# Scores of causal attention from two float32r parts, heads in pairs over the two partition halves

## What is computed

```
q = query @ wq + query @ Aq @ Bq * 4.0
k = query @ wk
v = query @ wv + query @ Av @ Bv * 4.0
q, k = apply_rope(q), apply_rope(k)
scores = einsum('bhqd,bhkd->bhqk', q, k) / sqrt(16)
scores = where(causal, -1e9, scores)
out = einsum('bhqk,bhkd->bhqd', softmax(scores), v) @ wo
x = layernorm(query + out)
h = butterfly(x @ W_exp + b_exp, up_weights)
h = butterfly(gelu(h + up_bias), down_weights)
x = layernorm(x + h @ W_con + b_con + down_bias)
```

## Time and profile before

| | us |
|---|---|
| median of 3 runs | 1386.56 |
| lowest, highest | 1382.6, 1386.81 |
| the profiled execution, its own time | 1382.2 |
| its span, first to last instruction | 1380.5 |
| TensorE busy | 1235.3 |
| VectorE busy | 1008.0 |
| ScalarE busy | 828.9 |
| GpSimd busy | 480.6 |

### The profile page before, as it was taken

One profiled execution on the slowest core, in us unless ns is written; L12 is line 12 of the kernel. 1 busy time (PEld: TensorE's weight loads), 2 busy tenths in 40 slices (PEclk: granted clock), 3 DMA queues, 4 the chain that ended last, 5 costly groups with the idle time before them and its releaser, 6 DMA issues.

```text
span 1380.5 us, 29447 instructions
## 1 busy us (share of the span) xinstructions
PE 1235.3 (89%) x9032; PEld 819.5 (59%) x9032; DVE 1008.0 (73%) x2182; ACT 828.9 (60%) x1291; POOL 480.6 (35%) x520
## 2 busy tenths in 40 slices
PE   3577899999999999999999989899999999989876
PEld 2434456666666666566666656566665656656465
DVE  5597977868686877868687877868687777857343
ACT  2266658575665748575674847575674847575612
POOL 3031433434343433334344333434243432432210
PEclk8788799999999999999999999999999999999988
DMA  4523342515334242524324342524324342432110
GB/s 160 148 69 111 100 133 75 167 49 156 95 102 125 84 147 63 154 71 141 107 76 134 93 147 65 153 76 131 117 71 139 93 146 59 145 91 87 39 49 16
DMA packets 97161, 144.24 MB, mean 104 GB/s; under 512 B 18392, under 2 KB 62936, under 8 KB 97120
## 3 DMA queue, kind: packets, MB, share of 16 engines
q1 hardware_dynamic: 96064, 140.85, 34.6%
q10 hardware_dynamic: 832, 1.83, 0.4%
q0 software_dynamic: 224, 1.04, 0.2%
HBM read 92.02 MB, written 51.64 MB: 104 GB/s over the span
## 4 chain that ended last, share of the span: by engine, by line
PE 61%; DVE 14%; issue 14%; DMA 4%; ACT 3%; POOL 2%; SPq 2%; DVEq 0%; POOLq 0%; ACTq 0%
PE ps_m L521 19%; PE ps_m L665 11%; PE ps_o L634 8%; PE ps_s L561 8%; PE ps_t L600 6%; PE ps_m L644 4%; DVE m_raw L862 3%; PE ps_s L569 3%; DMA qk_scr<-parts 2%; DVE x_res L955 2%; DVE rope_in L889 2%; PE ps_m L650 1%; DVE m_part L874 1%; DVE m_raw L865 1%; DMA k_st<-qk_scr 1%
## 5 line engine op out<-in xcount | busy, mean ns | idle before, releaser
L739 ACT ACTIVATE pT<-ps_t 128x512 f32<-128x512 f32 x640 | 362.9, 594 | 223.1 <-PE ps_t L600 222.3
L862 DVE TENSOR_REDUCE m_raw<-ps_s 128x1 f32<-128x512 f32 (+2 forms) x768 | 352.6, 502 | 98.3 <-PE ps_s L569 93.9
L1021 POOL TENSOR_SCALAR_AFFINE_SELECT pT<-pT 128x384 f32<-128x384 f32 (+1 forms) x320 | 178.9, 566 | 428.5 <-ACT pT L739 427.4
L561 PE MATMUL ps_s<-k_st,q_st 96*128 96x128 bf16 (+2 forms) x1536 | 250.6, 262 | 68.2 <-DVE m_raw L862 36.5
L561 PEld LDWEIGHTS ps_s<-k_st,q_st 96*128 96x128 bf16 x1536 | 118.3, 99 | 234.7 <-issue 94.0
L600 PE MATMUL ps_t<-q_st,k_st 99*128 99x512 bf16 (+3 forms) x1024 | 240.7, 310 | 7.5 <-ACT pT L739 4.8
L634 PE MATMUL ps_o<-pT,v_aug 128*32 128x512 f32 (+3 forms) x2048 | 197.0, 456 | 1.6 <-issue 1.6
L569 PE MATMUL ps_s<-maskb,identb 128*128 128x256 bf16 (+1 forms) x640 | 164.6, 257 | 0.0
L920 DVE TENSOR_TENSOR x1T_lo<-gact,x1T_hi 128x512 fp32r<-128x512 f32 x128 | 102.9, 814 | 45.7 <-ACT x1T_hi L792 45.7
L865 DVE TENSOR_REDUCE m_raw<-ps_s 128x2 f32<-128x512 f32 x128 | 87.4, 687 | 56.0 <-PE ps_s L569 54.6
L600 PEld LDWEIGHTS ps_t<-q_st,k_st 99*128 99x128 bf16 x1024 | 84.6, 100 | 73.2 <-issue 30.5
(11 more groups left out here) (122 smaller groups left out, 2145.5 us busy)
## 6 DMA issues: line engine op xcount, KB each, us to landing
qk_scr<-parts SPq DMA_DIRECT2D x32, 768.0 KB, 3.8
k_st<-qk_scr SPq DMA_DIRECT2D x384, 64.0 KB, 2.4
o_scr<-o_raw SPq DMA_DIRECT2D x64, 256.0 KB, 2.4
q_st<-qk_scr SPq DMA_DIRECT2D x64, 192.0 KB, 2.9
r_b<-in_xT SPq DMA_DIRECT2D x17, 512.0 KB, 3.8
q_st<-qk_scr SPq DMA_DIRECT2D x64, 128.0 KB, 3.0
o_c<-o_scr SPq DMA_DIRECT2D x32, 256.0 KB
r_b<-r_scr SPq DMA_DIRECT2D x32, 256.0 KB
```

The costliest lines, as they stand in the source:

```text
L561: return pe.matmul(ps_s[:, half, off:off + (k1 - k0)], q_st[0:NK, h, pos(qt) * P:(pos(qt) + 1) * P], k_st[0:NK, h, k0:k1], start=start, st ...
L739: act.activation(pT[:, g % 2, u, half * T:(half + 1) * T], ps_t[:, ST_BANK[n], :], ACT.Exp, scale=SCALE).then_inc(exp_done, 1)
L862: ins = dve.tensor_reduce(m_raw[:, pos(qt), u:u + 1], ps_s[:, half, off:off + cols], AX.X, ALU.max, negate=True)
L1021: pool.affine_select(out=v, in_=v, compare_op=ALU.is_ge, fill=0.0, base=0, pattern=[[0, 3 if u < GH else GH], [1, P]], channel_multiplier= ...
```

## The change

Queries and keys are split into two float32r parts, high and low, and three products are used: high with high, low with high, high with low. A head so has 48 rows (NK), and with two rows for the two parts of its maximum 50. Heads 0 to 7 stand in partitions 0 to 63 and heads 8 to 15 in partitions 64 to 127 of `q_st` and `k_st` (the weights' columns are reordered so that these are the even and the odd heads). A unit now holds a pair of heads, one in each half; its matmuls are issued in turn for r = 0 and r = 1, on rows 0 to 47 and 64 to 111, and write to two different banks. Units 0 and 2 of a group are key or query tile 3 of a pair (512 columns for each head), 1 and 3 the two other tiles (384 and 128), unit 4 the tile of 256 columns of both pairs. The counts of columns are the same as before. Both matmuls of a mask follow the pair; they still use all 128 rows.

Around it: both banks of S are now filled in one go, so S waits for all reductions of the unit before; ST waits once for both its banks; PV, XT, MT and W1 no longer stand between two halves of S or ST but before or behind them. The rotation's steps after `rot` are one rounding on ScalarE (HIGH) and one subtraction in place on GpSimd (LOW), and two DMAs write the parts (QKW, at steps 3 and 7 instead of 4 and 8); the rotation of the next half waits until these have landed. FILL has eight DMAs instead of nine. The maxima are split in two parts by two VectorE instructions into a padded tile `m_pad`, transposed by one float32 matmul of 128 columns, and read back by two DMAs instead of one. `pos` is gone, and the tokens stand in their own order. Two fills of ones (4096 float32 elements in 32 partitions each) replace one of 8192 bf16 elements.

```diff
-NPART = 3
-PRODUCTS = [(0, 0), (1, 0), (2, 0), (0, 1), (1, 1), (0, 2)]
-NK = len(PRODUCTS) * DH
+HP = H // 2
+GP = GH // 2
+ROWS = P // 2
+NK = 3 * DH
+NM = 2
...
-        put("ST", i, 2 * t)
         if t in first:
             put(*first[t])
...
-        put("ST", i, 2 * t + 1)
-
-        ahead = (i, 2 * (t + LEAD)) if t + LEAD < NU else (i + 1, 2 * (t + LEAD - NU))
-        put("S", *ahead)
-        if t in second:
...
+        put("ST", i, t)
+        put("S", *((i, t + LEAD) if t + LEAD < NU else (i + 1, t + LEAD - NU)))
+        for table in (second, third):
...
         if u >= 1:
             if g == 0:
                 put("PV", i - 1, 4 * (NG - 1) + u - 1)
...
-                put("PART0", i + 1, n)
-            if t == 3 * n + 3:
-                put("RES1", i + 1, n)
-            if t == 3 * n + 4:
-                put("PART1", i + 1, n)
-            if t == 4 * n + 4:
-                put("PART2", i + 1, n)
+                put("HIGH", i + 1, n)
+            if t == 4 * n + 3:
+                put("LOW", i + 1, n)
                 put("QKW", i + 1, n)
...
-        q_st = sb("q_st", [P, H, T], BF16)
-        k_st = sb("k_st", [P, H, T], BF16)
+        q_st = sb("q_st", [P, HP, T], F32R)
+        k_st = sb("k_st", [P, HP, T], F32R)
...
+                    wait(pe, max_done, 2 * (NU * b + n))
+
+                    def s_mm(r, off, x, qt, start):
+                        rows, pr = slice(ROWS * r, ROWS * r + NK), GP * g + x
+                        return pe.matmul(ps_s[:, r, off:off + (qt + 1) * P],
+                                         q_st[rows, pr, qt * P:(qt + 1) * P],
+                                         k_st[rows, pr, 0:(qt + 1) * P], start=start, stop=False,
+                                         skip_group_check=True)
...
+                    elif u % 2 == 0:
+                        for r in range(2):
+                            s_mm(r, 0, u // 2, 3, True)
+                    else:
+                        for r in range(2):
+                            s_mm(r, 0, u // 2, 2, True)
+                        for r in range(2):
+                            s_mm(r, 3 * P, u // 2, 0, False)
+
+                    for r in range(2):
...
+                        pe.matmul(o, identb[:, :], m, start=False, stop=True,
+                                  skip_group_check=True).then_inc(s_done, 1)
...
-                    wait(pe, exp_done, 2 * NU * b + ST_BEFORE[n] + 1)
...
+                    wait(pe, exp_done, 2 * NU * b + max(ST_BEFORE[2 * n:2 * n + 2]) + 1)
...
                 elif kind == "ROPE":
                     pool.wait_ge(evac["QK"], 4 * b + 2 * n + 2)
-                    wait(pool, p3_done, 2 * b + n)
+                    wait(pool, qk_out, DMA * 2 * (2 * b + n))
```

294 lines of the change are left out of this document (142 added, 152 removed).

## The result

The changed kernel is slower: 1546.88 us (median of 4, 1543.78 to 1549.84) against 1384.58 for the kernel before, a ratio of 1.117 (95% interval 1.114 to 1.121). The profiled execution took 1549.84 us, its span 1548.1. The forecast was 1343.

What follows compares the result with a forecast made beforehand. TensorE was taken as the bound: 2.7 us saved there plus 0.3 less 0.5 of new waits gives 2.5 per batch, 40 in sixteen; with 3 at the start, 1382.2 becomes 1339, or 1343 against the median; range 1303 to 1396.

Steps and rivals of the forecast that it cites:

- What bounds the kernel now: Whole kernel: TensorE, busy 89% of the span, bounds it, so its saved time mostly comes off the batch.
- TensorE's terms: Score work per group of four heads: 5.83 us before, 5.16 after, saving 0.67, or 2.7 us per batch.
- Entry 0.19: Going into a half-array pair: 0.11 us for the change of form plus 0.08 for the exposed weight load.
- 77% of the promise of a pair: Paired score columns: 2.13 us would stream in 2.77, 0.64 more per group, leaving about no change.
- no overlap: Rival, score pairs: the halves stream one after the other, 136 us more, about 1480 us; chance 0.10.
- loads in line: Rival, score pairs: the halves' weight loads go one after the other, 59 us, 1385 to 1402 us; chance 0.11.
- the slow 128 columns: Rival: float32r pairs of 128 columns take 0.22 us instead of 0.12, 26 us more, 1369 us; chance 0.08.
- the reductions become the bound: Rival: seven units per batch wait for the single set of score banks, 3 us per batch, 1383 us; chance 0.08.
- The fills: SP's queue: eight instead of nine fill DMAs of the same bytes, hidden; a fill 2 to 3 us late is covered.
- The new wait: Score banks, steps 7, 9, 10, 14: the next pair waits for all the last one's reductions, 0.5 us per batch net.
- The 0.3 saved elsewhere: Split of the maxima and dropped VectorE subtraction: 0.3 us per batch off TensorE's 3 us of waits.
- The start: Before the first scores: two of four operations between rotation and write fall away, saving 3 us.

Runs made afterwards that it cites:

- two copies: Changed kernel with the repeating high-part query fill replaced by two DMAs of 16 rows each: 1428.1 us, 1.032 of the kernel before.
- fastest: Changed kernel with two row copies, GpSimd subtraction halved, V at steps 10 and 14, early gelu splits, SP's queue reordered, group 3's fill at step 1: 1354.6 us.
- the version with halves: Changed kernel with two row copies, maxima transposes and last W1 behind PV, V at steps 10 and 14, GpSimd subtractions at 3 and 7 halved: 1388.5 us.
- the short ones: Reductions reading only 64 columns (32 in the fifth unit): 1370.9 us on the 1388.5 us version with halved GpSimd subtractions, 1351.6 on the kernel before.

## Why the prediction was wrong

**The account.** A batch runs from the first matmul of the output projection to that of the next batch. In ten batches of the middle, TensorE's records (where they overlap counted once) are its own time, with what they hold at the lower clock level counted half; the other half is lost to the clock, and the rest of the batch is idle. For the kernel before this gives 72.9 to 73.2 us for every batch, whether it ran at full clock or not. A delay shorter than the overlap of two records stays in the own time.

| us per batch | before | changed | two copies | fastest |
|---|---|---|---|---|
| TensorE's own time at full clock | 73.0 | 69.8 | 69.9 | 70.8 |
| idle | 3.8 | 12.4 | 8.3 | 5.3 |
| lost to the lower clock | 1.3 | 6.4 | 3.5 | 0.3 |
| batch | 78.1 | 88.6 | 81.7 | 76.4 |

So the forecast's main term was nearly right: it had 2.7 us saved on TensorE, and the changed kernel has 3.2. Against it stand 8.6 us more idle and 5.1 more lost to the clock, for which the forecast had 0.2 net and nothing. About half of each (4.1 and 2.9) goes with the repeating DMA. The fastest version, with more dense products behind PV, saves 2.2, idles 1.5 more and loses 1.0 less to the clock.

The scores with their masks and transposes take 22.0 us in it instead of 25.3 (batches at full clock), PV 10.8 instead of 10.7, the dense products with the transposes of x 38.1 instead of 37.1. Twelve dense products stand right behind PV there, eleven with the two copies, and the first matmul of one ends 0.43 us behind PV for 512 columns and 0.32 for 256, 0.20 more than their pitch; before, behind ST, it was 0.23 and 0.17.

**What bounds the kernel now** failed in its last step, "a microsecond taken from TensorE's own work is, for the most part, a microsecond off the batch". TensorE was busy 95% of the middle, but between steps 3 and 12 two strings of round trips in SP's queue (rotation, write, fills; output, sums, reciprocals, output projection) had little slack. The kernel before shows it itself when its reductions are cut short: its waits for the output projection grow from 4.7 to 9.0 us in 600, those for the fills from 1.6 to 6.8. The forecast saw these intervals in the chain as "issue" and took them for covered.

**The clock** was put at nothing, without a reason. An idle stretch costs more than itself where the granted clock falls behind it: 5.1 us per batch more than before in the changed kernel, 2.2 with the two copies.

**TensorE's terms** were right or too careful, one by one. Pair of 512 in 0.24: right (0.23). Partner at 0.01: right (3 ns). 128 columns at 0.12: 0.055 to 0.06, the rate of bf16. Exit into the masks 0.11: right (0.215 instead of 0.11 for 256 columns). Entry 0.19: right (0.20). The sum comes near by luck, though, since its errors nearly cancel. The score work before was priced at 23.3 us per batch and took 25.1 to 25.3, mostly since the matmul of S behind PV is 0.10 late, sixteen times a batch. That after was priced at 20.6 and takes 22.0, about 1.2 of it in small delays of S, some behind reductions, that leave no gap. And the dense work, 1.0 more, was left out. The loss that the prediction estimated from the Trainium skill, TensorE: Matmul & The Clock Gate, Part 3 (77% of the promise of a pair) didn't appear: partners overlap wholly here. Nor did the rivals of no overlap, of loads in line (two loads take 0.19) and of the slow 128 columns. That the reductions become the bound is spoken against, for the version with halves, by the short ones, which gain less there than before.

**The fills** are the step that failed most: "The queue of SP carries eight instead of nine fill DMAs of the same bytes in longer pieces ... and these transfers are hidden." Bytes and issues were counted, and on how many engines a DMA lies was not. The two fills with a repeat in each group cost 119 us: TensorE's waits for the keys were 123.9 us in all instead of 27.6. The fill that was named as possibly late, but covered, is the one of step 3. In the changed kernel its reader at step 7 waits 1.0 to 2.2 us per batch, and the longer wait, 3.5 to 3.8 us, is at step 12, for the fill of step 8; in the later versions step 12 is the one that stays.

**GpSimd** "swaps one subtraction for one of as many elements": true, but it moved from step 8 to 7, and there holds VectorE's split of the maxima for 2.21 us instead of 0.176. That is 38 us in the version with two copies.

**The new wait** of 0.5 per batch was right for what shows as idle: waits for reductions grew from 1.6 to 3.4 us per batch with the two copies, those before the layer norm and the output projection fell by 1.2, as told: 0.6 net. What it costs with the clock behind it is more, for V at steps 10 and 14 took 31 us off. The steps named are those where it shows (7, 9, 10, 14). **The 0.3 saved elsewhere** were not: the shorter split was the one held by GpSimd.

**The start.** The first scores come at 44.29 us with two copies, 3.9 earlier than the earlier trace rows; with the repeat at 51.95, 3.8 later. 3 was right without it.

The expectation of the two copies (1340 to 1375) had the same fault as the prediction. Only with edits of order that the prediction doesn't have, in SP's queue above all, did the change come under the kernel before: 1354.6, 11 us over the forecast. That doesn't make the forecast right, since for the kernel before only two orders were tried. The rest is in the 1.5 us per batch that the fastest version idles more than the kernel before; it wasn't followed further.

## What to carry to other kernels

For each DMA that a change adds or rewrites, look at the slowest dimension of both sides, not at its bytes: an outermost repeat of two costs more than two DMAs, and what is queued behind pays with it. When an engine that is busy 95% is relieved, ask for every stretch where it already waits a microsecond what chain of round trips ends there, because the saving can stop at the first of them; a string of serial DMAs and issues of 0.4 us in one queue is such a chain. Price idle stretches with the clock that falls behind them. And when a step of GpSimd is moved, lay it beside what VectorE does at that time, the tiny instructions on the way to TensorE first.

## What the runs showed of the hardware

- Float32r matmuls of 48 to 50 rows in the two halves of the array overlap wholly, in streaming (a pair of 512 columns in 0.23 us) and in weight loads (two in 0.19); a float32r pair of 128 columns takes 0.055 to 0.06 us.
- Going from full-array float32r or from PV into such a pair costs 0.20 us, from the pair into full-array bf16 masks 0.105.
- A full-array float32r product behind the 32-column tiles of PV is 0.20 us late, a bf16 matmul of 96 rows 0.10; a float32r product behind the full-array bf16 scores of the kernel before was 0 to 0.05 late.
- With a DMA whose source begins with a repeat of 2, two packets are in flight at a time; the fill that was followed takes 7.8 us instead of 2.7, and a write behind it in the queue lands in 7.2 instead of 2.4 us.
- A VectorE subtraction of 16 elements per partition with both inputs in SBUF took 2.21 us beside a GpSimd subtraction of 2.34 that began 0.16 us earlier, and 0.176 in most places.
- TensorE busy for 2.42 of 4 us was followed by 4 us at a granted clock of 0.50. Per batch, 12.4 us idle came with 6.4 lost to the lower level, 8.3 with 3.5, 3.8 with 1.3; but 5.3 with 0.3 in the fastest version, so where the idle time lies counts too.
